# A Flamingo block on one core: the last two batches of the attention are finished in another way, and the first gate product is issued before a turn

## The chip, the cores and the metric

One core of one Trainium2 chip runs the whole program. The metric is the device time in microseconds of one execution, as the median of several runs. Engines: PE (matrix), DVE (vector), ACT (scalar), POOL (GpSimd), SP (issues DMAs).

## The reference, cut to what matters

x and ctx are (16, 256, 256), so there are 16 batches of 256 tokens and 256 features; 16 heads of 16.

```python
q = _layernorm(x) @ Wq.T + bq;  k = ctx @ Wk.T + bk;  v = ctx @ Wv.T + bv
attn = softmax(q k^T / 4)                  # per head
x = x + tanh(g_xattn) * ((attn v) @ Wo.T + bo)
h = act_qdq(_layernorm(x))                 # scale from the maximum over the whole tensor
up, gate = act_qdq(h @ W_up.T), act_qdq(h @ W_gate.T)
gate = act_qdq(gate * fixed_qdq_u16(sigmoid(gate)))
x = x + tanh(g_ffn) * (act_qdq(gate * up) @ W_down.T)
```

The maximum over the whole tensor in the first act_qdq is what splits the program in two: no gate product can start before the attention of all 16 batches and their second layernorm are done.

## The kernel before, in words

The program has two blocks with a barrier between them: `attention` (lines 29 to 810) and `feed_forward` (lines 892 on).

**Order of the attention.** Every engine walks through the same numbered steps g from -40 to 158, eight steps to a batch (`STEPS`, `batch(g, off)`: a task with offset off is done for batch b at step 8b + off). Nothing else sets the order; semaphores only make one engine wait for another. Scores for batch b are done one batch ahead, twice: `s_ps` (line 438, for the row maximum, taken on DVE in line 715) and, transposed, `st_ps` (line 453), which ACT turns into exponentials (line 606). From step 120 on there are no more `s_ps` scores, from step 128 on no more exponentials: the steps after that are the tail. Matmul inputs are split into a high and a low f16 part, so a product of two 256-wide operands (`split_product`) is 6 matmuls per 128 rows, 12 for a batch.

**The end of a batch.** `values` (line 412) multiplies the exponentials with the values at steps 2, 4, 6 and 8; each head takes 32 rows of `pv_ps`, 16 with its output, one with its denominator, 15 empty. ACT copies the two halves to `ot` at steps 5 and 9 (`take`, line 553). Then, for each batch b:

- step 10, SP: DMA of the denominators' rows from `ot` to `den` (line 336);
- step 12, DVE: reciprocal `rec` (line 753);
- step 14, SP: `rec` to DRAM (line 347), four DMAs that pack the second half's 16-row pieces of `ot` into the empty rows of the first (line 352), a DMA that reads the reciprocals from DRAM, each spread over 16 rows, into `recb` (line 357), and the load of `xr` (line 362);
- step 18, POOL: `at` = `ot` * `recb` (line 852); step 20, ACT: its f16 high part `ah` (line 632); step 21, DVE: the low part `al` (line 757);
- step 22, POOL: `xb`, the residual with the bias (line 868); step 23, PE: the output projection (line 467); step 24, DVE: `y` (line 725), SP: the store of y; step 25, DVE: statistics (lines 730, 735); step 26, POOL: `rstd` (lines 815, 817) and the normalised `lnall` (line 859), which is on DVE for the last two batches (line 742); step 30, DVE: the maximum (line 760).

After the last step the maximum over the partitions goes over PE twice (lines 542, 544) to `lmaxall` (line 809), and the barrier follows.

**Weights of the feed-forward.** They are quantised in pieces along the steps, turned on PE (`turn_weights`, 12 turns of 6 transposes each, through `s_ps`) and copied out by ACT (`keep_weights`, line 573), four at steps 131 and 132, four at 137, four at 139. A turn waits until the copy two before it is done.

**Start of the feed-forward.** DVE makes integers of `lnall` (line 1221), PE turns them (`turn`, line 1001), ACT and DVE split them (lines 1079, 1227); `gate(c, d)` on PE waits for the split of chunk c, turns chunk c + 2 and issues three pairs of products (line 1011) per chunk of two batches.

## Time and profile before

| | us |
|---|---|
| median of 3 runs (632.51 to 634.73) | 632.62 |
| the profiled execution | 634.7 |
| its span in the trace | 632.9 |
| PE busy | 567.9 (90%) |
| DVE busy | 486.7 (77%) |
| ACT busy | 437.5 (69%) |
| POOL busy | 202.0 (32%) |
| barrier between the blocks, about | 348 |

A row of the timeline has the start, the duration of the whole row, the engine, the line, the operation, output and input, and how many instructions it merges; in brackets stands the idle time ahead of it and what ended it. A row of windows has the length, then the busy time and the number of instructions for each engine, and PEclk, the granted clock of TensorE as a share of 2.4 GHz: 1.00 is 2.4 GHz and 0.50 is 1.2 GHz.

### The profile page before, as it was taken

What the parts mean: (1) busy time and instruction counts of PE and PEld (TensorE: products, weight loads), DVE (VectorE), ACT (ScalarE), POOL (GpSimd) and SP (SyncE); (2) the same over time, 40 slices, a digit from 0 to 9 for tenths busy, and PEclk for the clock granted to TensorE, in tenths of its full rate; (3) what the DMA queues carried; (4) which work ended last, traced back from release to release, by engine and by line L of the source; (5) the groups of instructions that cost most, each with busy time, mean ns of one, the idle gap of its engine ahead of it and who ended that gap; (6) DMA issues with size and microseconds to landing.
All of it is one profiled execution on the core that took longest, in us unless ns stands there. A gap on an engine that the chain in (4) does not pass through costs nothing. (4 is left out here: it accounts for less than half of the span.)

```text
span 632.9 us, 11543 instructions
## 1 busy us (share of the span) xinstructions
PE 567.9 (90%) x4271; PEld 338.0 (53%) x4271; DVE 486.7 (77%) x797; ACT 437.5 (69%) x629; POOL 202.0 (32%) x219
## 2 busy tenths in 40 slices
PE   2679999899999999999873799999999899949997
PEld 1346666566565666665442444434444344428886
DVE  5677889999999999898644298896888799964441
ACT  2226888678787787887762244437999998869960
POOL 4622347766665777653452000000000000010000
PEclk9879999999999999999986799999999999969999
DMA  6422444445435444333231000000000000013332
GB/s 189 126 85 76 129 127 129 120 138 143 147 112 136 141 128 110 111 106 106 63 83 54 2 1 0 1 1 0 1 0 1 1 1 0 1 66 101 135 134 99
DMA packets 42951, 49.12 MB, mean 78 GB/s; under 512 B 10640, under 2 KB 30480, under 8 KB 42896
## 3 DMA queue, kind: packets, MB, share of 16 engines
q1 hardware_dynamic: 41312, 43.81, 23.8%
q0 software_dynamic: 1152, 4.19, 2.1%
q8 instruction: 34, 0.56, 0.4%
q10 hardware_dynamic: 432, 0.39, 0.2%
q14 instruction: 21, 0.17, 0.1%
HBM read 24.58 MB, written 8.72 MB: 53 GB/s over the span
## 5 line engine op out<-in xcount | busy, mean ns | idle before, releaser
L715 DVE TENSOR_REDUCE negm<-s_ps 128x2 f32<-128x512 f32 x256 | 163.7, 682 | 28.2 <-PE s_ps L438 27.5
L606 ACT ACTIVATE pt<-st_ps 128x512 f32<-128x512 f32 x256 | 138.7, 596 | 56.1 <-PE st_ps L453 55.0
L1011 PE MATMUL pairs<-xq,wut 128*128 128x512 f16 x576 | 126.0, 379 | 6.5 <-DVE cmax L1276 3.4
L1011 PEld LDWEIGHTS pairs<-xq,wut 128*128 128x128 f16 x576 | 55.5, 98 | 77.0 <-DVE cmax L1276 7.3
L438 PE MATMUL s_ps<-kst,qst 96*128 96x256 f16 x512 | 82.9, 280 | 10.8 <-DVE negm L715 5.6
L453 PE MATMUL st_ps<-qst,kst 97*128 97x512 f16 x256 | 77.4, 383 | 0.8 <-ACT pt L606 0.8
L420 PE MATMUL pv_ps<-pt,vt 128*32 128x256 f32 x1024 | 68.5, 385 | 1.4 <-ACT ot L557 0.7
L1383 POOL PARTITION_ALL_REDUCE vmax<-vmax x5 | 1.8, 370 | 204.7 <-DVE vmax L1231 129.8
L1011 PE MATMUL pairs<-xq,wgt 128*128 128x512 f16 x288 | 65.0, 385 | 0.4 <-DVE xq L1227 0.3
L438 PEld LDWEIGHTS s_ps<-kst,qst 96*128 96x128 f16 x512 | 46.8, 99 | 34.0 <-DVE negm L715 21.2
L826 POOL TENSOR_SCALAR xn<-xt,mv,rstd 128x256 f32<-128x256 f32 x30 | 36.5, 1223 | 64.6 <-PE misc L518 64.4
L1064 PE MATMUL pairs<-wdt,h 128*128 128x256 f16 x384 | 48.9, 279 | 8.4 <-ACT h L1171 8.4
L1089 ACT COPY gb<-pairs 128x1024 f32<-128x1024 f32 x24 | 24.3, 1012 | 41.6 <-PE pairs L1011 41.6
L420 PEld LDWEIGHTS pv_ps<-pt,vt 128*32 128x32 f32 x1024 | 26.9, 109 | 38.7 <-issue 25.3
L1011 PEld LDWEIGHTS pairs<-xq,wgt 128*128 128x128 f16 x288 | 28.1, 99 | 34.6 <-issue 2.0
L1064 PEld LDWEIGHTS pairs<-wdt,h 128*128 128x128 f16 x384 | 38.3, 100 | 14.1 <-issue 8.8
L1283 DVE CUSTOM_DVE_ANT_0 gb<-lnall 128x1024 f32<-128x1024 int16 x24 | 29.1, 1217 | 13.5 <-ACT lnall L1118 13.5
L550 ACT ACTIVATE qk<-misc,bqk_s 128x256 f16<-128x256 f32 x64 | 26.9, 473 | 18.2 <-PE misc L381 18.2
L1244 DVE TENSOR_REDUCE cmax<-gb 128x1 f32<-128x3072 f32 (+1 forms) x10 | 27.1, 2710 | 15.5 <-ACT gb L1089 15.5
L859 POOL TENSOR_SCALAR lnall<-y,mv,rstd 128x256 f32<-128x256 f32 x28 | 34.0, 1221 | 1.5
L1367 DVE SCALAR_TENSOR_TENSOR lnall<-pairs,scal,lnall 128x512 f32<-128x512 f32 x16 | 11.9, 749 | 26.5 <-PE pairs L1064 26.5
L1135 ACT ACTIVATE lnall<-pairs,scal 128x1024 int16<-128x1024 f32 x24 | 26.5, 1112 | 6.4 <-PE pairs L1011 6.3
(164 smaller groups left out, 1026.7 us busy)
## 6 DMA issues: line engine op xcount, KB each, us to landing
qst<-qk SPq DMA_DIRECT2D x96, 64.0 KB, 2.1
kst<-qk SPq DMA_DIRECT2D x45, 128.0 KB, 3.2
xt<-in_x SPq DMA_DIRECT2D x16, 256.0 KB, 4.3
ct<-in_ctx SPq DMA_DIRECT2D x16, 256.0 KB, 3.1
recb<-rec_dram SPq DMA_DIRECT2D x16, 256.0 KB
xr<-in_x SPq DMA_DIRECT2D x16, 256.0 KB, 4.0
out<-y SPq DMA_DIRECT2D x16, 256.0 KB, 4.0
lnall<-out POOLq DMA_DIRECT2D x8, 512.0 KB, 4.3
```

The costliest lines, as they stand in the source:

```text
L420: mm = nc.tensor.matmul(pv_ps[32 * c:32 * c + 32, u % 2, :], vt[:, b % 3, kt, 8 * (c // 2) + 2 * u + c % 2, :], pt[:, u % 2, c // 2, kt, c ...
L438: mm = nc.tensor.matmul(s_ps[tt][:, r, :], qst[0:96, b % 3, r, j, tt * P:(tt + 1) * P], kst[0:96, b % 3, j, :], start=True, stop=True)
L453: nc.tensor.matmul(st_ps[u % 3][:], kst[:, b % 3, j, kt * P:(kt + 1) * P], qst[:, b % 3, :, j, :], start=True, stop=True).then_inc(st_done, 1)
L550: op = nc.scalar.activation(qk[:, 2 * i, e, :], frm[:, e, :], ACT.Identity, bias=bqk_s[:, i, e:e + 1])
L606: nc.scalar.activation(pt[:, (j // 2) % 2, j % 2, kt], st_ps[u % 3][:], ACT.Exp, scale=1.0 / (WS * WS * HD ** 0.5)).then_inc(exp_done, 1)
L715: nc.vector.tensor_reduce(negm[:, b % 2, tt, lo:lo + 5:4], s_ps[tt][:], AX.X, ALU.max, negate=True).then_inc(max_done, 1)
L826: op = nc.gpsimd.tensor_scalar(xn[:, tt, :], xt[:, b % 3, tt, :], mv[:, tt, 0:1], rstd[:, tt:tt + 1], ALU.subtract, ALU.mult)
L859: nc.gpsimd.tensor_scalar(t["lnall"][:, b, tt * D:(tt + 1) * D], y[:, b % 2, tt, :], mv2[:, tt, 0:1], rstd2[:, tt:tt + 1], ALU.subtract, A ...
L1011: mm = nc.tensor.matmul(ps[:, p, k, :], w[:, a, dt, f * P:(f + 1) * P], xq[:, b, c, dt, :], start=n == 0, stop=n == len(terms) - 1)
L1064: mm = nc.tensor.matmul(ps[:, 2 + d, b, tt * D:(tt + 1) * D], lh, wdt[:, h, f, :], start=n == 0, stop=n == len(terms) - 1)
L1244: nc.vector.tensor_reduce(cmax[:, 0, n:n + 1], tile, AX.XY, ALU.max).then_inc(g_max, 1)
L1283: nc.vector.tensor_tensor_reduce(gb[:, c, 2 * p:2 * p + 2].rearrange("p f w -> p (f w)"), ia[:, d, 2 * p:2 * p + 2].rearrange("p f w -> p ...
```

## The change

Batches are counted from 0; LAST is 15, END is step 128.

1. **Batch 15 without DMAs.** Its denominators no longer go through `den`, DRAM and `recb`. For each half v, PE multiplies four 128-column pieces of `ot` with four columns of the identity (`turn_den`), which puts the denominators on the partitions; DVE takes the reciprocal of 16 columns and copies it 32 wide (`rec_of`); PE turns that back (`turn_rec`, four f32 matmuls with 128 columns) into PSUM, spread over the rows; DVE multiplies it with `ot` (`attended`). Halves are not packed: each is cast (`high_last`, ACT; `low_last`, DVE) and projected by itself (`project_last`, 12 matmuls for each half) with a copy of Wo that has zeros in the rows without output (`wo16`). `y` and its statistics are made in two pieces.
2. **`wo16`** is prepared at steps 80 to 87 on POOL: a memset of 1024 columns and eight DMAs from POOL's queue, one per step.
3. **Batch 14.** SP packs it at step 122, right behind the load of `den`, ahead of the store of `rec` and the load of `recb` (step 123). POOL multiplies at step 127, ACT casts at step 128 ahead of `take(15, 1)`, DVE's low part and PE's projection follow at 128 and 129.
4. **Weights.** Turns 0 and 1 go between `turn_den(1)` and `turn_rec(1)`, turns 2 to 9 behind `project_last(1)`, turns 10 and 11 behind the first product of the final maximum. They go through `st_ps`. ACT's copies stand in the same order.
5. **Order on DVE at the end.** Normalising and maximum of batch 14 stand behind the statistics of batch 15; `mv2`, `ve2`, `rstd2` have two buffers.
6. **Feed-forward.** In `gate(0)` the first pair of products is issued before `turn(2, 0)`.

```diff
+            def store_rec(b): ...
+            def pack(b):
+                sp.wait_ge(den_loaded, 16 * (b + 1))
+                if b >= 2:
+                    sp.wait_ge(at_done, b - 1)
+                for c in range(4):
+                    sp.dma_start(ot[32 * c + HD:32 * c + 32, b % 2, 0], ot[32 * c:32 * c + HD, b % 2, 1]
+                                 ).then_inc(packed[b % 2], 16)
+            def spread_rec(b): ...
...
-                if (b := batch(g, 10)) is not None:
+                if (b := batch(g, 10)) is not None and b < LAST:
...
+                if g == END - 6:
+                    pack(LAST - 1)
+                if g == END - 5:
+                    store_rec(LAST - 1)
+                    spread_rec(LAST - 1)
...
+            def turn_den(v):
+                pe.wait_ge(ot_taken, 2 * LAST + v + 1)
+                frm = ot[:, LAST % 2, v].rearrange("p u q -> p (u q)")
+                for c in range(4):
+                    mm = nc.tensor.matmul(den_ps[:, 64 * v + 4 * c:64 * v + 4 * c + 4], frm[:, c * P:(c + 1) * P],
+                                          ident[:, HD:P:32], start=True, stop=True)
+                mm.then_inc(den_turned, 1)
+            def turn_rec(v):
+                pe.wait_ge(rec_wide, v + 1)
+                pe.wait_ge(at_last, v)
+                for c in range(4):
+                    mm = nc.tensor.matmul(recb_ps[:, c * P:(c + 1) * P], recx[:, c * P:(c + 1) * P], ident[:],
+                                          start=True, stop=True)
+                mm.then_inc(rec_spread, 1)
+            def project_last(v):
+                terms = [(x, w, k) for x, w in ((ahl[v], 0), (ahl[v], 1), (all_[v], 0)) for k in range(2)]
+                pe.wait_ge(ah_last, v + 1)
+                for first in range(2):
+                    if first == 1:
+                        pe.wait_ge(al_last, v + 1)
+                    for tt in range(KT):
+                        for m, (x, w, k) in list(enumerate(terms))[4 * first:4 + 2 * first]:
+                            mm = nc.tensor.matmul(last_ps[tt], x[:, k, tt * P:(tt + 1) * P], wo16[:, v, w, k, :],
+                                                  start=v == 0 and m == 0, stop=v == 1 and m == len(terms) - 1)
+                        if v == 1 and first == 1:
+                            mm.then_inc(o_last, 1)
...
+                if g == END - 2:
+                    pe.wait_ge(max_done, UNITS * NB)
+                    turn_den(0)
+                if g == END - 1:
+                    turn_rec(0)
...
-                if g in (PREP + 11, PREP + 12): ...
-                if g in (PREP + 17, PREP + 19): ...
+                if g == END + 1:
+                    project_out(LAST - 1, bank(PAIRS * (LAST - 1) + PROJ), g)
+                    turn_den(1)
+                    pe.wait_ge(ident16_set, 1)
+                    pe.wait_ge(exp_done, UNITS * NB)
+                    for k in range(2):
+                        turn_weights(0, k)
+                    turn_rec(1)
+                    pe.wait_ge(wo16_set, 128)
+                    project_last(0)
+                    project_last(1)
+                    for n in range(2, 10):
+                        turn_weights(n // 4, n % 4)
             pe.wait_ge(lmax_done, 1)
             pe.wait_ge(ot_taken, 2 * NB)
             nc.tensor.transpose(pv_ps[0:1, 0, 0:P], lmax[:], ident[:]).then_inc(lmax_turned, 1)
+            for k in range(2, 4):
+                turn_weights(2, k)
...
+                if g == END:                                  # ACT
+                    high_of(LAST - 1)
                 if (b := batch(g, 9)) is not None:
                     take(b, 1)
...
+                if g == END + 1:
+                    high_last(0)
+                    keep_weights(0, 0)
+                    keep_weights(0, 1)
+                    high_last(1)
+                    for n in range(2, 12):
+                        keep_weights(n // 4, n % 4)
...
+                if g == END - 1:                              # DVE
+                    rec_of(0)
+                if g == END:
+                    low_of(LAST - 1)
+                    attended(0)
+                if g == END + 1:
+                    rec_of(1)
+                    low_last(0)
+                    y_of(LAST - 1)
+                    attended(1)
+                    stats_of(LAST - 1)
+                    low_last(1)
+                if g == END + 7:
+                    for tt in range(KT): ...                  # y and bn_stats of each piece
+                    gather_stats(LAST)
+                    ln_last(LAST - 1)
+                    ln_max(LAST - 1)
+                    ln_last(LAST)
+                    ln_max(LAST)
...
+                if g == 80:                                   # POOL
+                    nc.gpsimd.memset(wfall[:].rearrange("p n t d -> p (n t d)")[:, 0:4 * D], 0.0).then_inc(wo16_zeroed, 1)
+                if 80 <= g < 88:
+                    v, c = divmod(g - 80, 4)
+                    pool.dma_start(wo16[32 * c:32 * c + HD, v], wo2[32 * c + HD * v:32 * c + HD * v + HD]).then_inc(wo16_set, 16)
...
             def gate(c, d):
                 pe.wait_ge(xt_low, c + 1)
-                if ahead(c, 2):
+                if c and ahead(c, 2):
                     turn(c + 2, d)
                 for p in range(PR):
+                    if c == 0 and p == 1:
+                        turn(2, 0)
                     pe.wait_ge(g_kept, PR * c + p + 1)
                     products(wgt, c, p).then_inc(g_done, 1)
```

## Rows read from the trace of the kernel before

**Rows 1.** Busy time by stretch: four windows (us), granted clock, DMA share, GB/s.

```profile
211.00:228.40 17.40, 17.40 (x169) 11.39 (x167) 15.96 (x34) 13.49 (x29) 12.38 (x14) 1.00 0.51 145
...
330.00:332.00 2.00, 1.21 (x18) 0.90 (x15) 1.69 (x5) 1.58 (x3) 0.00 (x0) 0.98 0.61 95
336.00:338.00 2.00, 0.00 (x0) 0.00 (x0) 1.71 (x3) 0.86 (x2) 1.49 (x2) 0.73 0.00 0
356.00:358.00 2.00, 2.00 (x7) 0.74 (x6) 0.00 (x0) 0.00 (x0) 0.00 (x0) 0.65 0.00 0
```

**Rows 2.** Timeline of PE at the end of the attention block.

```profile
327.19 0.58 PE L381 MATMUL misc<-woh,ah 128*128 128x256 f16 x2 [1.25 <-DVE al L757]
...
338.82 0.58 PE L381 MATMUL misc<-woh,ah 128*128 128x256 f16 x2 [3.31 <-DVE al L757]
...
346.21 0.37 PE L542 MATMUL pv_ps<-ident,lmax 128*1 128x128 f32 x1 [4.68 <-DVE lmax L805]
```

**Rows 3.** Timeline of DVE at the end of the attention block.

```profile
326.31 0.63 DVE L757 TENSOR_TENSOR al<-at,ah 128x512 f16<-128x512 f32 x1
...
336.30 1.67 DVE L742 TENSOR_SCALAR lnall<-y,mv,rstd 128x256 f32<-128x256 f32 x2 [4.53 <-POOL rstd L817]
...
341.58 0.75 DVE L725 SCALAR_TENSOR_TENSOR y<-misc,tgs,xb 128x512 f32<-128x512 f32 x1 [2.42 <-PE misc L381]
...
344.50 0.73 DVE L742 TENSOR_SCALAR lnall<-y,mv,rstd 128x256 f32<-128x256 f32 x2 [1.10 <-POOL rstd L817]
...
347.57 0.16 DVE L809 COPY lmaxall<-pv_ps 128x1 f32<-128x1 f32 x1 [0.67 <-PE pv_ps L544]
```

**Rows 4.** Timeline of ACT at the end of the attention block.

```profile
323.31 0.59 ACT L557 COPY ot<-pv_ps 128x512 f32<-128x512 f32 x1 [1.47 <-PE pv_ps L420]
...
325.17 0.64 ACT L632 CAST ah<-at 128x512 f16<-128x512 f32 x1
...
330.42 2.98 ACT L573 COPY wut<-s_ps 128x768 f16<-128x768 f16 x4 [3.21 <-PE s_ps L409]
```

**Rows 5.** Timeline of SP's queue, the last batch but one.

```profile
313.54 0.59 SPq L336 DMA_DIRECT2D den<-ot  x1
316.01 0.32 SPq L347 DMA_DIRECT2D rec_dram<-rec  x1
316.43 2.45 SPq L352 DMA_DIRECT2D ot<-ot  x4
318.99 0.66 SPq L357 DMA_DIRECT2D recb<-rec_dram  x1
```

**Rows 6.** DMA issues from 300 to 345 us: KB each, median us to landing.

```profile
rec_dram<-rec SPq DMA_DIRECT2D x3, 16.0 KB, 1.4
```

**Rows 7.** Timeline of POOL, the last two batches.

```profile
323.37 1.27 POOL L852 TENSOR_TENSOR at<-ot,recb 128x512 f32<-128x512 f32 x1 [3.88 <-DMA recb<-rec_dram]
...
336.23 1.26 POOL L868 TENSOR_TENSOR xb<-xr,tbo 128x512 f32<-128x512 f32 x1
```

**Rows 8.** Line 496: weight loads of its f32 matmuls, duration min/median/max ns, first and last start.

```profile
L496 PEld LDWEIGHTS pv_ps<-wof,bvw x4: 186/190/190, 19.0 to 19.5; 128*128 128x128 f32 x4
```

**Rows 9.** Line 776 on DVE: a copy with a broadcast input, duration min/median/max ns.

```profile
L776 DVE COPY bvw<-bvc x1: 1384/1384/1384, 17.5 to 17.5; 128x256 f32<-128x256 f32 x1
```

**Rows 10.** Timeline of all engines where the feed-forward block starts.

```profile
349.97 1.89 PE L1001 MATMUL pairs<-ident,h 128*128 128x128 f16 x16 [2.44 <-DVE h L1221]
...
352.09 0.69 DVE L1227 TENSOR_TENSOR xq<-pairs,xq 128x1024 f16<-128x1024 int16 x1 [1.39 <-ACT xq L1079]
...
353.59 1.01 PE L1001 MATMUL pairs<-ident,h 128*128 128x128 f16 x8 [1.73 <-DVE h L1221]
```

**Rows 11.** Line 1392: software DMA issues on POOL, min/median/max ns.

```profile
L1392 POOL DMA_DIRECT2D lnall<-out x8: 722/722/1021, 561.3 to 617.2; - x8
```

**Rows 12.** Timeline of POOL and PE in the steady state, near step 80.

```profile
228.62 1.15 POOL L846 TENSOR_TENSOR cl<-ct,ch 128x512 f16<-128x512 f32 x1
...
232.03 0.38 PE L381 MATMUL misc<-ch,wh_k 128*128 128x256 f16 x2
```

More of the change, by code:

```diff
@@ L466, in _ @@
                     mm.then_inc(v_done, 1)
[L467 to L478 removed]
+                if (b := batch(g, PROJ)) is not None and b < LAST - 1:
+                    project_out(b, bank(g), g)
                 if (b := batch(g, Q)) is not None:
@@ L628, in _ @@
                     nc.scalar.copy(ch[:], ct[:, b % 2]).then_inc(ch_done, 1)
-                if (b := batch(g, 20)) is not None:
-                    act.wait_ge(at_done, b + 1)
-                    act.wait_ge(o_done, b)
-                    nc.scalar.copy(ah[:], at[:, b % 2]).then_inc(ah_done, 1)
+                if (b := batch(g, 20)) is not None and b < LAST - 1:
+                    high_of(b)
                 if g == -13:
@@ new lines, in low_of, with rec_row, ln_last @@
+            def low_of(b):
+                dve.wait_ge(ah_done, b + 1)
+                dve.wait_ge(o_done, b)
+                nc.vector.tensor_tensor(al[:], at[:, b % 2], ah[:], ALU.subtract).then_inc(al_done, 1)
+            def rec_row(b):
+                dve.wait_ge(den_loaded, 16 * (b + 1))
+                if b:
+                    dve.wait_ge(rec_written, 16 * b)
+                nc.vector.reciprocal(rec[:], den[:]).then_inc(rec_done, 1)
+            def ln_last(b):
+                dve.wait_ge(rstd2_done, b + 1)
+                for tt in range(KT):
+                    nc.vector.tensor_scalar(t["lnall"][:, b, tt * D:(tt + 1) * D], y[:, b % 2, tt, :], mv2[:, b % 2, tt, 0:1],
+                                            rstd2[:, b % 2, tt:tt + 1], ALU.subtract, ALU.mult).then_inc(ln_done, 1)
@@ L738, in _ @@
                     low(0, bank(PAIRS * b + Q), ql_done)
-                if (b := batch(g, 26)) is not None and b >= NB - 2:
-                    dve.wait_ge(rstd2_done, b + 1)
-                    for tt in range(KT):
-                        nc.vector.tensor_scalar(t["lnall"][:, b, tt * D:(tt + 1) * D], y[:, b % 2, tt, :], mv2[:, tt, 0:1],
-                                                rstd2[:, tt:tt + 1], ALU.subtract, ALU.mult).then_inc(ln_done, 1)
                 if (b := batch(g, -29)) is not None and b >= 3:
@@ new lines, in _ @@
+                if (b := batch(g, 30)) is not None and b < LAST - 1:
+                    ln_max(b)
+                if g == END - 1:
[10 more added lines that the diff above has]
+                    low_last(1)
```

237 lines of the change are left out of this document (147 added, 90 removed).

## The prediction

> **What bounds the kernel now.** I read the page's slices first, then windows, then the timeline of each engine from 310 to 360 us, where nearly all of the change lies. In the steady state PE has no gap at all: 17.40 us busy of 17.40 for one batch, with POOL at 12.38 [rows 1]. What matters there is only whether PE is made to wait. In the tail no engine is full; a chain of hand-overs decides. Look at PE: it sits idle for 1.25 us ahead of the projection of batch 14 and 3.31 us ahead of that of batch 15, each time waiting for the low part from DVE, and 4.68 us ahead of the final maximum [rows 2]. Behind the waits stands a DMA: POOL waited 3.88 us for `recb` of batch 14 [rows 7]. From the last copy of `pv_ps` (323.31 + 0.59 = 323.90) [rows 4] to the projection of batch 15 (338.82) [rows 2] it takes 14.9 us, for some 6 us of work. From there to the end of the last DVE operation, 347.57 + 0.16 = 347.73 [rows 3], it is 8.9 us, and the barrier follows. Whatever moves the last engine's end at this barrier moves the whole feed-forward by as much. TensorE's clock is the second thing to see: after the gap behind the weight turns it falls to 1.2 GHz (0.73 between 336 and 338) and is back at 2.4 GHz only between 356 and 358; after the shorter gap at 326 it had fallen as well, since two matmuls took the same 0.58 us at 327.19 as at 338.82 [rows 2], and from 330 to 332 it was up again at 0.98 [rows 1].
>
> **Batch 14, the new start of the chain.** `den` was issued at 313.54 and the reciprocal was there when `rec` was issued at 316.01; the four packs took SP 2.45 us and `recb` went out at 318.99 [rows 5]. Now the packs come first: they can start when `den` has landed, about 315.65, and hold SP until 318.1. Only then does the store of `rec` go, lands 1.4 us later [rows 6] at about 319.6, and `recb` follows at 319.65, 0.65 us later than before. Before, 323.37 - 318.99 = 4.4 us passed until POOL had it [rows 5, 7]; I take the same, since `xr` still follows at once. So POOL starts at 324.0 instead of 323.37 and ends at 325.3. (Bounds: without the packs' traffic beside it `recb` could land 1 us sooner; it could also land 1 us later.) ACT casts, 0.64 us [rows 4], until 325.95, and only then does `take(15, 1)`, 0.59 us, until 326.5. PE's side reaches that point by about 325.4: `turn_den(0)` and `turn_rec(0)` add some 3 us to its queue ahead of `values(15, 3)`, and ACT's wait covers them by 0.5 us; without that cover they would cost up to 1 us. DVE's low part takes 0.63 us [rows 3], so PE's projection of batch 14 starts at 326.8 (before 327.19, [rows 2]). At 1.2 GHz its twelve matmuls start 0.213 us apart (338.82 to 341.4 for the other one, y begins at 341.58, [rows 2, 3]), so it ends at 329.4.
>
> **Batch 15, second half.** `turn_den(1)`: four f32 matmuls are eight passes, since line 496 shows four weight loads for two matmuls, 0.19 us each [rows 8]. 8 x 0.19 = 1.5, and 0.2 until it can be read: 331.1. Reciprocal 0.3. The copy 32 wide is 512 columns from one source; the nearest rows are 0.73 / 2 = 0.37 us for 256 columns of one-source work [rows 3] and 1.384 for a 256-column copy with a broadcast input [rows 9]. Lower end 0.6, upper 2 x 1.38 = 2.8. I take 0.9, nearer to the lower end, since it is the same kind of work, with something added because POOL is at work on batch 13's `lnall` here: 332.4. `turn_rec(1)` 8 x 0.19 + 0.15: 334.1. `attended(1)` 0.7: 334.9. ACT casts until 335.5; DVE has the statistics of batch 14 (1.05 us) in between and has the low part at 336.65. PE has done `project_last(0)` and two thirds of `project_last(1)` by then (about 1.3 and 0.9 us if the clock is up since 330, as it was before) and needs four more matmuls: the last starts at about 337.1, and both pieces are there at 337.45. Before, that point was 341.58 [rows 3]. So the join comes **4.1 us earlier**.
>
> **What is late next.** `y`, statistics, aggregation, the root on POOL (1.10 us of idle on DVE, [rows 3]) and the maximum took 347.73 - 341.58 = 6.15 us. Now batch 14's normalising and maximum (0.73 + 0.69) fall into the root's wait and stick out by 0.4, and batch 13's maximum adds 0.3 ahead of y. How long such work takes beside POOL is open: the two normalising operations of batch 14 took 1.67 us together, beginning at 336.30 beside POOL's `xb` (336.23, 1.26 us), those of batch 15 only 0.73; `al` took 0.63 at 326.31, with POOL at work too [rows 3, 7]. In my sum that does not matter yet (rival E prices it), because another chain ends later: **the weights**. Before, turns and copies lay inside the waits and cost nothing. Now ten of twelve copies come after `project_last(1)`. One is 2.98 / 4 = 0.745 us on ACT [rows 4]. From 337.15: first turn 0.5, ten copies 7.45, end 345.1. DVE's chain would end at 337.45 + 6.15 + 0.7 = 344.3, and 0.3 more because the last small matmul stands behind turn 11 in PE's queue: 344.6. So ACT ends the block at 345.1 against 347.73: **-2.6 us**.
>
> **Feed-forward.** PE waited for the integers of chunk 2 and started its turn at 353.59, though DVE's split for chunk 0 was done at 352.09 + 0.69 = 352.78 [rows 10]. With the product first, PE works from 352.82: **-0.77 us**. The turn itself is the same work later. If the clock rises at the same moment whatever PE does, half of that is lost (-0.4).
>
> **Steady state.** POOL gets a memset (about 0.9) and eight DMA issues of 0.72 to 1.02 us [rows 11]: 6.7 to 9.1 us against 17.40 - 12.38 = 5.0 us of idle per batch [rows 1]. It runs 1.7 to 4.1 us late and recovers in the next batch. Who waits: `cl` is done at 229.77 and PE needs it at 232.03 [rows 12], 2.26 us of slack against 0.9 + 0.72 ahead of it. I take 0; upper end 2.
>
> **Sum.** -2.6 - 0.8 = -3.4 us. Against the profiled execution, 634.7 (span 632.9), that is 631.3 (span 629.5). The median of the runs shown is 632.62, 2.1 us below that execution, so the forecast is **629.2 us**.
>
> **Rivals.**
> - *A, the join comes late.* The clock stays at 1.2 GHz from 326.8 to the join, which makes `turn_den`, `turn_rec` and the two last projections about 2.6 us longer; a wide copy near its upper end or a late `recb` would do the same. Everything behind moves with it: 345.1 + 2.6 = 347.7, where the block ended before, and only the feed-forward's 0.8 is left: **631.8**. For it: PE idles until 326.8, and the clock was down in that place [rows 2]. Against: it rose after that with PE as busy as here.
> - *B, the clock stays up.* Weight turns fill PE until the barrier, as they did up to 336 when it was at 2.4 GHz. If it is still up at the first turn, the 3.8 us from 353.59 to about 357.4 at 1.2 GHz take 1.9, and the first turns 0.4 less: **627.0**. Against: about 2.9 us of PE idle around the barrier (its last matmul near 344.4, its first turn 349.97 - 347.73 = 2.24 us behind the last engine's end, [rows 3, 10]), and the clock fell in the gap after 336 [rows 1].
> - *C, slower: POOL's software DMAs.* Place: steps 80 to 87. If an issue holds POOL 2 us and more instead of 0.72, POOL is 8 x 2 + 0.9 = 16.9 us fuller, 11.9 beyond its idle time, and PE waits for `cl` and the `at` chain for all but 2.3 of it: +9.6 - 3.4, **638.8**. It makes the kernel slower from 1.2 us per issue on. For it: the only price is that of another shape [rows 11].
> - *D, POOL's lateness is paid once.* The issues cost what the row shows, but `cl` or the `at` chain has less slack than I think and PE waits for the upper end of 2 us: **631.2**.
> - *E, DVE is held by POOL and its chain ends the block.* If normalising batch 14 beside POOL's root takes 1.67 instead of 0.73 us (+0.9), and the wide copy and the low part ahead of the join are held for another 0.6 together, DVE ends at 344.6 + 1.5 = 346.1 instead of ACT at 345.1: **630.2**. For it: 1.67 beside `xb`; against: `al` at 0.63 [rows 3, 7]. The Trainium skill (GPSIMD Engine Reference, Specifications) says that POOL's SBUF interfaces are shared with VectorE, with contention for DVE instructions in a two-port mode or with two SBUF inputs. By that rule both kinds of work are held here and E is what comes; by the row of `al` only the normalising is, and the sum stays as it is. The trace agrees for one of the two kinds.
>
> **Chances.** Forecast 0.44 (own range 627.9 to 630.6), A 0.18, B 0.12, C 0.06, D 0.10, E 0.10. No change can be told within 0.5%, 3.16 us, so the forecast lies just beyond that line; of its 0.44 I give 0.27 to faster, 0.17 to same, and of E 0.03 and 0.07. Faster 0.27 + 0.12 + 0.01 of A + 0.03, same 0.17 + 0.17 + 0.10 + 0.07, slower 0.06. The range runs from B with some spread, 626.3, to A and D with theirs, 632.7.
>
> **What would show it.** Steps: `at` of batch 14 at 324 and not before 323.4; `take(15, 1)` behind the cast; y of batch 15 near 337.5; ten ACT copies of 0.745 us in a row as the last thing before the barrier; PE's products 2.85 us after its first turn. Wrong: if DVE or PE ends the block, if `values(15, 3)` is later than ACT's cast, if the copy 32 wide takes over 1.5 us, if PE shows gaps between 228 and 250 us, or if the granted clock is 1.00 at the first turn of the feed-forward.

## Result and the profile after

The changed kernel takes **626.91 us** (median of 4 runs, 624.88 to 627.51) against 632.57 us before (median of 4 runs, 632.18 to 634.73). The ratio is 0.9899, 95% interval 0.9875 to 0.9923. That is faster by over 0.5%, but the gain is 5.7 us where the sum said 3.4. The time lies inside the whole range of the forecast (626.3 to 632.7), yet outside the forecast's own (627.9 to 630.6): it falls in the part that belonged to rival B, and rival B's condition, a clock that is still up at the first turn of the feed-forward, was not met. So that it is inside is luck. Of all the runs below one, 632.52 us of the kernel e4, was in a slower state and is left out of that kernel's ratio.

The two profiled executions differ by more, 632.9 and 623.0 us of span, and one has to see first how much of these 9.9 us the change can have made. I cut both at the same events. The work ahead of the first copy of `pv_ps` ended 3.55 us earlier, though the change touches none of it: over all profiles below that point lies anywhere between 54.6 and 59.4 us, 58.35 before and 54.80 after (last section). From there to the end of batch 9 it took 0.8 us less (170.47 and 169.64). Nothing of the change is known to act there, yet the three profiles of kernels with the old tail (before, e1, e5) have 170.3 to 170.5 us and the eleven others 169.6 to 170.1, with no overlap. Some 0.5 us of it may therefore belong to the change in a way that no run explains. What is left lies where the change acts:

| stretch (us) | before | after | difference |
|---|---|---|---|
| batches 10 and 11 | 35.13 | 36.26 | +1.13 |
| issue of `den` (14) to first DVE operation of the feed-forward | 35.01 | 30.06 | -4.95 |
| from there to the end | 284.35 | 282.66 | -1.69 |

Their sum, -5.5, fits the medians, with the 0.5 us or without. One profile of each kernel is a thin base for the last line: over the six profiles of kernels with the changed feed-forward and no idle matmuls (after, a0, e2, e3, e6, e7) it is 282.7 to 283.7 us, 283.2 in the mean, so the gain there is nearer to 1.2 than to 1.7 us. First the windows of the kernel after, which answer to [rows 1]: length, busy time and number of instructions of PE, PEld, DVE, ACT, POOL, then granted clock, DMA share and GB/s.

```profile
222.40:239.80 17.40, 17.21 (x165) 11.24 (x165) 16.39 (x35) 13.99 (x31) 15.48 (x19) 1.00 0.47 132
239.80:257.20 17.40, 16.81 (x163) 11.12 (x156) 15.26 (x34) 13.93 (x30) 13.56 (x16) 1.00 0.42 121
...
322.00:324.00 2.00, 0.00 (x0) 0.00 (x0) 0.81 (x1) 1.10 (x2) 1.73 (x2) 1.00 0.70 201
340.00:342.00 2.00, 0.46 (x5) 0.46 (x6) 1.59 (x4) 0.00 (x0) 0.00 (x0) 0.62 0.02 4
344.00:346.00 2.00, 1.60 (x4) 0.58 (x5) 2.00 (x5) 0.54 (x1) 0.00 (x0) 0.50 0.00 0
346.00:348.00 2.00, 2.00 (x8) 0.76 (x7) 0.28 (x1) 0.00 (x0) 0.54 (x1) 0.67 0.00 0
348.00:350.00 2.00, 2.00 (x17) 1.17 (x16) 0.00 (x0) 1.01 (x1) 0.00 (x0) 1.00 0.00 0
```

Three things are to be seen. PE, gapless in [rows 1], lacks 0.19 and 0.59 us in the two batches in which POOL issues the new DMAs. The clock stays at 2.4 GHz (1.00) through the whole tail, also in the window in which PE did nothing. It falls only at the barrier and is back about 7 us behind the first DVE operation of the feed-forward (340.34), where before it took 9 us from 348.55 [rows 1].

PE's timeline at the end, which answers to [rows 2] (start, duration, engine, line, operation, idle time ahead and what ended it):

```profile
324.53 0.60 PE L416 MATMUL misc<-wo,ah 128*128 128x256 f16 x4 [2.63 <-DVE al L830]
...
325.84 0.95 PE L478 MATMUL s_ps<-ident,ot 128*128 128x4 f32 x8
326.65 0.83 PE L444 MATMUL st_ps<-ident,wut 128*128 128x128 f16 x12
327.88 1.16 PE L486 MATMUL s_ps<-ident,wi 128*128 128x128 f32 x8 [0.40 <-DVE wi L813]
...
331.36 0.39 PE L499 MATMUL misc<-wfall,cl 128*128 128x256 f16 x2
...
331.81 0.83 PE L444 MATMUL st_ps<-ident,wut 128*128 128x128 f16 x12
...
341.54 1.89 PE L1179 MATMUL pairs<-ident,h 128*128 128x128 f16 x16 [2.32 <-DVE h L1401]
344.40 4.18 PE L1189 MATMUL pairs<-xq,wgt 128*128 128x512 f16 x12 [0.98 <-DVE xq L1407]
```

The projection of batch 14 (324.53) lasts 1.31 us until `turn_den(1)` at 325.84, at 2.4 GHz; I had 2.6. DVE and ACT in the same stretch, for [rows 3] and [rows 4]:

```profile
323.19 1.09 DVE L830 TENSOR_TENSOR al<-at,ah 128x512 f16<-128x512 f32 x1 [2.39 <-ACT ah L662]
...
326.83 0.26 DVE L809 RECIPROCAL recl<-s_ps 128x16 f32<-128x16 f32 x1 [1.01 <-PE s_ps L478]
327.18 0.65 DVE L813 COPY wi<-recl 128x512 f32<-128x512 f32 x1
...
329.08 0.69 DVE L819 TENSOR_TENSOR at<-ot,s_ps 128x512 f32<-128x512 f32 x1
...
331.82 0.47 DVE L913 SCALAR_TENSOR_TENSOR y<-misc,tgs,xb 128x256 f32<-128x256 f32 x1
...
333.81 0.70 DVE L841 TENSOR_SCALAR lnall<-y,mv,rstd 128x256 f32<-128x256 f32 x2
...
339.26 0.16 DVE L971 COPY lmaxall<-pv_ps 128x1 f32<-128x1 f32 x1 [1.40 <-PE pv_ps L623]
```

```profile
322.54 0.62 ACT L662 CAST ah<-at 128x512 f16<-128x512 f32 x1 [2.94 <-POOL at L1014]
323.06 0.58 ACT L636 COPY ot<-pv_ps 128x512 f32<-128x512 f32 x1
...
332.35 1.50 ACT L652 COPY wgt<-st_ps 128x768 f16<-128x768 f16 x2 [1.92 <-PE st_ps L444]
333.82 2.98 ACT L652 COPY wut<-st_ps 128x768 f16<-128x768 f16 x4
336.77 2.98 ACT L652 COPY wdt<-st_ps 128x768 f16<-128x768 f16 x4
```

`take(15, 1)` stands behind the cast, as foreseen. The join (y of batch 15, first piece) is at 331.82. DVE has the last maximum at 339.42, 7.60 us behind it; ACT's copies run without a gap until 339.75, 7.93 us behind it. So ACT ends the block, as the sum had it, and DVE is 0.3 us from doing so.

SP and POOL (batch 14), for [rows 5] and [rows 7]:

```profile
310.28 0.59 SPq L376 DMA_DIRECT2D den<-ot  x1
312.60 2.46 SPq L330 DMA_DIRECT2D ot<-ot  x4
315.10 0.58 SPq L323 DMA_DIRECT2D rec_dram<-rec  x1
316.79 0.66 SPq L337 DMA_DIRECT2D recb<-rec_dram  x1
```

```profile
321.24 1.27 POOL L1014 TENSOR_TENSOR at<-ot,recb 128x512 f32<-128x512 f32 x1 [4.42 <-DMA recb<-rec_dram]
322.46 1.27 POOL L1019 TENSOR_TENSOR xb<-xr,tbo 128x512 f32<-128x512 f32 x1
```

`recb` goes out 6.51 us behind `den`, against 5.45 before, and POOL starts at 10.96 against 9.83.

### The profile page after: what moved, and what is told of

The parts are those of the page before. It is cut to its first block and busy times, and to the rows that moved or that the text cites. A ratio compares the mean times of both kernels' runs of the same rounds, so it can differ in the third digit from the quotient of the medians.

```text
span 623.0 us, 11662 instructions
## 1 busy us (share of the span) xinstructions
PE 565.0 (91%) x4315; PEld 338.5 (54%) x4315; DVE 488.8 (78%) x804; ACT 438.4 (70%) x630; POOL 206.7 (33%) x227
## 5 line engine op out<-in xcount | busy, mean ns | idle before, releaser
L695 ACT ACTIVATE pt<-st_ps 128x512 f32<-128x512 f32 x256 | 138.8, 596 | 54.6 <-PE st_ps L531 53.5
L516 PE MATMUL s_ps<-kst,qst 96*128 96x256 f16 x512 | 81.1, 275 | 11.0 <-DVE negm L872 7.2
L1502 DVE TENSOR_TENSOR gb<-lnall 128x1024 f32<-128x1024 int16 x24 | 29.1, 1215 | 2.4 <-ACT lnall L1319 2.4
```

Source lines behind the costliest of these rows:

```text
L516: mm = nc.tensor.matmul(s_ps[tt][:, r, :], qst[0:96, b % 3, r, j, tt * P:(tt + 1) * P], kst[0:96, b % 3, j, :], start=True, stop=True)
L695: nc.scalar.activation(pt[:, (j // 2) % 2, j % 2, kt], st_ps[u % 3][:], ACT.Exp, scale=1.0 / (WS * WS * HD ** 0.5)).then_inc(exp_done, 1)
L1502: nc.vector.tensor_tensor(gb[:, c, 2 * p:2 * p + 2], ia[:, c % 2, 2 * p:2 * p + 2], ib[:, c % 2, 2 * p:2 * p + 2], ALU.mult).then_inc(p3_d ...
```

## The experiments

Each run's profile was cut at the same events. In this table of the tail the times count from the issue of `den` for batch 14, in us. The last line is the stretch from the feed-forward's first DVE operation to the end.

| | before | after | a0 | e3 | e6 | e4 | e5 | b2 |
|---|---|---|---|---|---|---|---|---|
| `recb` issued | 5.45 | 6.51 | 6.66 | 5.45 | 6.62 | 6.12 | 5.45 | 5.46 |
| `at` (14) starts | 9.83 | 10.96 | 10.37 | 9.42 | 10.95 | 10.03 | 9.26 | 9.67 |
| `take(15, 1)` starts | 9.77 | 12.78 | 12.21 | 13.19 | 12.79 | 11.87 | 9.76 | 11.51 |
| join | 28.04 | 21.54 | 20.97 | 20.21 | 21.56 | 20.63 | 26.41 | 20.29 |
| first DVE op. of feed-forward | 35.01 | 30.06 | 29.48 | 28.72 | 28.93 | 29.14 | 33.09 | 28.10 |
| rest of the program | 284.35 | 282.66 | 283.21 | 283.74 | 283.42 | 280.15 | 285.74 | 280.97 |

The join is the first operation of the last `y`. The names in the table are those of the runs below. Each ratio is taken against runs of the kernel before that were made at the same time (medians 633.4, 633.72 and 633.0 us for three groups of kernels). No run puts back the main edit alone, batch 15 without DMAs; what it brings is read from the chain in the profiles.

**The changed kernel again.**

> The changed kernel once more, as the anchor for the others. Theory: its gain is in three places, tail of the attention about -5.0 us (from the issue of den of batch 14 to the first DVE operation of the feed-forward, 30.1 us against 35.0), feed-forward about -1.7, and POOL's DMAs in batches 10 and 11 +1.1, so 626.9 in the median. The 3.55 us that its first profiled execution was ahead before the first copy of pv_ps (54.80 against 58.35) belong to the clock at the start and not to the change: here the first copy should lie anywhere between 54 and 60 us. Rival: they belong to the change (nothing in it acts before step 80), then the first copy is at 54.8 again and the median nearer to 624.

Measured: 626.9 us (6 runs), ratio 0.9902 (0.9875 to 0.9929). The tail is the first profile's within 0.6 us, the difference being when `recb` landed. So the clock that is up at the projection of batch 14 is no accident of one execution: it was at 2.4 GHz there in all eleven profiles of the changed kernel and of its variants. The clock came back 7.7 us behind the first DVE operation of the feed-forward, not 7.0, and the rest of the program took 283.21 us.

**Only the order of the feed-forward**, in the kernel before:

```diff
-                if ahead(c, 2):
+                if c and ahead(c, 2):
                     turn(c + 2, d)
                 for p in range(PR):
+                    if c == 0 and p == 1:
+                        turn(2, 0)
```

> The kernel before with only the feed-forward part of the change: the first pair of products ahead of turn(2, 0). Theory: PE starts its products right behind DVE's split, 0.77 us sooner, and since the clock is at 1.2 GHz there for some time behind the start it wins 0.4 to 0.8: 631.9 to 632.2. Rival: PE's work only swaps places and the later turn holds chunk 2, no gain within 0.2 us.

Measured: 632.33 us (12 runs), ratio 0.9984 (0.9967 to 1.0002), that is -1.0 us and hardly told from nothing. Its profile shows why this term is less than it looks: the windows about its first product (PE's work from 350 us) are

```profile
350.00:352.00 2.00, 2.00 (x6) 0.65 (x5) 1.72 (x4) 0.00 (x0) 0.77 (x1) 0.50 0.00 0
352.00:354.00 2.00, 2.00 (x6) 0.71 (x5) 0.00 (x0) 0.00 (x0) 0.00 (x0) 0.50 0.00 0
354.00:356.00 2.00, 2.00 (x14) 1.12 (x13) 0.00 (x0) 0.81 (x1) 0.00 (x0) 0.69 0.00 0
356.00:358.00 2.00, 2.00 (x11) 0.94 (x10) 0.00 (x0) 0.20 (x1) 0.00 (x0) 1.00 0.00 0
```

PE works without a gap, but at 1.2 GHz, and DVE's first maximum over the products came 16.39 us behind the first DVE operation, against 16.34 before, with the clock back at +9.7 instead of +8.8. The loss from the later rise is half of 0.9, so by this working, which no run separates, the order itself gives about 0.4 us.

**POOL's DMAs.** In one kernel they were spread, two at a time, over steps 83 to 107, with the memset at 83; in another they were left out (the memset stays, so batch 15 is projected with zeros and the output is not the reference's).

```diff
-                if 80 <= g < 88:
-                    v, c = divmod(g - 80, 4)
+                if g in (83, 91, 99, 107):
+                    for n in ((g - 83) // 4, (g - 83) // 4 + 1):
+                        v, c = divmod(n, 4)
```

> The eight DMAs that fill wo16 go two at a time to steps 83, 91, 99 and 107, just ahead of the place where POOL waited 4.6 us for PE, with the memset at 83. Theory: POOL's lateness in steps 80 to 88 makes PE wait once, 1.1 us in all between the copies of batches 10 and 11; spread out it costs nothing, so 1.1 us faster than the changed kernel, 625.8. Rival: the 1.1 us come from elsewhere (load of the queue, a phase of PE and DVE), then the same time as the changed kernel within 0.3 us.

> The changed kernel without the eight DMAs from POOL's queue that fill wo16 (the memset stays, so the last batch is projected with zeros and its output is not the reference's). Theory: these DMAs hold POOL for 6 us in batch 10 and the PE waits once for it, so the stretch from the second copy of batch 9 to that of batch 11 goes from 36.26 back to 35.13 us and nothing is paid later: 1.1 us faster than the changed kernel. Rival: spread over four batches they only moved the loss behind batch 11 (50.5 instead of 49.6 us up to den), so it is a loss of phase between PE and DVE that comes back wherever POOL is late, and it is gone here altogether; if even here the stretch or the one behind it is long, it is not the DMAs.

Measured: spread 626.46 us (6 runs), ratio 0.9900 (0.9872 to 0.9927); left out 625.53 us (4 runs), 0.9877 (0.9855 to 0.9899). Without the DMAs batches 10 and 11 take 35.13 us, as before, and the stretch behind them 49.59, again as before. Spread, the first is 35.13 but the second 50.50: the cost had moved, 0.9 us of it, not gone. (b1, which has this edit too, takes 50.90 there; the twelve kernels without it 49.6 to 50.2, so that stretch varies by some 0.6 us by itself.) The medians of the three kernels can't be told apart; it is the stretches that show the cost. How it comes about is seen on POOL in the changed kernel, behind batch 10:

```profile
236.55 2.42 POOL L988 TENSOR_SCALAR xn<-xt,mv,rstd 128x256 f32<-128x256 f32 x2 [0.74 <-PE misc L591]
238.92 1.07 POOL L1047 DMA_DIRECT2D wfall<-wo  x2
240.01 1.28 POOL L1036 TENSOR_TENSOR xb<-xr,tbo 128x512 f32<-128x512 f32 x1
```

and then on DVE and on PE of the same kernel:

```profile
241.38 0.75 DVE L789 SCALAR_TENSOR_TENSOR y<-misc,tgs,xb 128x512 f32<-128x512 f32 x1 [1.29 <-issue]
```

```profile
228.00 0.38 PE L416 MATMUL misc<-ch,wh_k 128*128 128x256 f16 x2 [0.19 <-POOL cl L1008]
...
242.19 0.39 PE L416 MATMUL misc<-xh,wh_q 128*128 128x256 f16 x2 [0.59 <-DVE y L789]
```

Without the DMAs PE has no such wait from 224 to 245 us, and the same operations stand so (POOL, then DVE):

```profile
238.45 1.27 POOL L1036 TENSOR_TENSOR xb<-xr,tbo 128x512 f32<-128x512 f32 x1
```

```profile
239.81 0.75 DVE L789 SCALAR_TENSOR_TENSOR y<-misc,tgs,xb 128x512 f32<-128x512 f32 x1 [0.20 <-issue]
```

Two issues stand between `xn` and `xb`. Counted from the second copy of batch 9, `xb` starts 1.44 us later with them (15.57 and 14.13). DVE's y needs `xb` and starts 0.09 us behind its end in both kernels, and PE's next product needs the bank that y reads. This chain had less slack than `cl`, for which PE waited only 0.19 us. The two gaps make 0.78 of the 1.13 us; where the other 0.35 lie I can't show.

**Packing batch 14 behind the store again:**

```diff
-                if g == END - 6:
-                    pack(LAST - 1)
                 if g == END - 5:
                     store_rec(LAST - 1)
+                    pack(LAST - 1)
                     spread_rec(LAST - 1)
```

> Only the order on SP's queue for batch 14 is put back: the reciprocals are stored first, then the four packs, then recb. Theory: packing first delays recb from 5.45 to 6.51 us behind den, and the whole chain hangs on it: at of batch 14 starts 10 us behind den instead of 10.96, the join and the barrier come about 1 us earlier, 625.9. Rival: recb lands when the packs' traffic is through, whatever is issued first, or take(15, 1) is held by PE's values at 321.9 instead; then within 0.3 us of the changed kernel.

Measured: 626.14 us (6 runs), ratio 0.9894 (0.9866 to 0.9921), not told from the changed kernel. The profile tells more: `recb` goes out at 5.45 again, `at` starts 1.0 to 1.5 us earlier and the join comes 0.8 to 1.3 earlier than in the two profiles of the changed kernel. It is not the whole 1.5, because now PE's side of `take(15, 1)` is late: in this execution the clock was down for 3.4 us, and PE took 1.94 us for what had been 1.07 (first line). `values(15, 3)` (second line) then ended at 325.16, and `take(15, 1)` started at 325.23. It began 12.05 us behind `den` instead of 10.55; in e2, which packs first but whose clock fell in the same place, it is 12.05 as well, so this lateness goes with the clock and not with the edit.

```profile
318.91 1.94 PE L454 MATMUL pv_ps<-pt,vt 128*32 128x256 f32 x16
...
324.09 1.07 PE L454 MATMUL pv_ps<-pt,vt 128*32 128x256 f32 x16
```

So packing first bought nothing here; it cost about 1 us of chain. In the profiled execution what was gained in the tail was lost again behind it: the feed-forward's clock came back 8.5 us behind its first operation instead of 6.95, and the rest took 283.74 us. Whether that holds for the other runs, whose median did not move, is not shown.

**Half of the weights ahead of the join** (PE's part; ACT's copies follow the same order):

```diff
                 if g == END - 1:
+                    turn_weights(0, 0)
+                    turn_weights(0, 1)
                     turn_rec(0)
...
+                    turn_weights(0, 2)
+                    turn_weights(0, 3)
                     project_out(LAST - 1, ...)
                     turn_den(1)
-                    for k in range(2):
-                        turn_weights(0, k)
+                    turn_weights(1, 0)
+                    turn_weights(1, 1)
                     turn_rec(1)
...
-                    for n in range(2, 10):
+                    for n in range(6, 12):
```

> The changed kernel with six of the twelve weight turns and copies in ACT's gaps: two ahead of turn_rec(0), two ahead of the projection of batch 14, two behind turn_den(1); the other six behind project_last(1), none behind the final transpose. Theory: the ten copies of 0.74 us behind the join end the block at 339.75 and DVE's chain would end at 338.3; with six left (4.5 us) DVE decides: 1.4 us faster than the changed kernel, 625.5. Rival: the copies delay the casts on ACT's queue, or the turns the values of batch 15 on PE, by as much: no gain within 0.3 us.

Measured: 627.0 us (6 runs), ratio 0.9898 (0.9878 to 0.9918). The block does end earlier: with six copies left ACT is done 4.97 us behind the join, DVE's chain 6.54 (7.60 in the changed kernel, since PE's small matmuls no longer stand behind a turn), and the feed-forward starts 7.37 us behind the join, where the changed kernel and the five variants that keep its ten copies and its small matmuls (a0, e2, e3, e4, e7) all have 8.51 or 8.52.

```profile
335.80 2.98 ACT L654 COPY wdt<-st_ps 128x768 f16<-128x768 f16 x4
```

But PE's last weight turn now ends at 337.94, 3.2 us ahead of the feed-forward's first operation; the clock falls 2.4 us ahead of that operation instead of with it, and is back at +7.9. The rest of the program took 283.42 us, 0.8 longer than in the first profile of the changed kernel but only 0.2 longer than in its second, so that the gain is given back in this way is likely and not shown; the median says only that it is not there. What is shown is that the weights ended the block and that the chain on DVE is right behind them.

**Idle matmuls at the barrier.** They compute nothing that is read:

```diff
+            def idle_work(n):
+                for i in range(n):
+                    nc.tensor.matmul(ps[:, 2, 0, :], wgt[:, 0, 0, 0:P], wut[:, 0, 0, 0:CW], start=True, stop=True)
+            idle_work(5)
             turn(0, 0)
             turn(1, 1)
+            idle_work(5)
```

> Five idle 512-column matmuls of no use ahead of the first turn of the feed-forward and five behind the second, into a bank that is not in use yet. Theory: the clock falls to 1.2 GHz at about 340.5, 1.3 us after PE's last work, and is back at 347.3; filling the gaps from 340.2 on keeps it up, and half of the time that PE works at 1.2 GHz (about 1.0 us of turns and 2.9 us of products) comes back: 1.5 to 1.9 us faster, 625.2. Rival: the gap around the barrier (339.25 to 340.3) cannot be filled and is enough to drop the clock; then the idle matmuls run at 1.2 GHz and delay the first turn by up to 0.9 us: 627.5, with the clock back a little sooner.

> Idle matmuls as in the kernel that filled the gaps at the start of the feed-forward, and two more behind the last small matmul of the attention, under ACT's last copy. Theory: the clock never falls around the barrier, the first reduction of the feed-forward starts 13.1 us behind its first DVE operation instead of 15, and what is behind it is the same; from the first DVE operation to the end 280.2 us against 282.7 to 283.2: 2.7 us faster than the changed kernel, 624.2, in every execution. Rival: the clock falls in some executions all the same, then the idle matmuls delay the first turn and the time is as unsteady as before.

Measured: 626.21 us (6 runs), ratio 0.9871 (0.9841 to 0.9900); with two more behind the last small matmul of the attention (e8), 624.43 us (4 runs, 623.84 to 624.79), ratio 0.9861 (0.9839 to 0.9882). In both profiles the clock stays at 1.00 over the barrier, the first maximum over the products comes 13.12 us behind the first DVE operation instead of 14.95, and the rest of the program takes 280.15 and 280.78 us. In all four profiles in which idle matmuls kept the clock up (e4, e8 and, below, b2 and b3) it takes 280.2 to 281.6 us, in the six profiles of the same code without them 282.7 to 283.7. The window at the start of the feed-forward, with the first five of them (e4):

```profile
344.00:346.00 2.00, 1.59 (x12) 0.78 (x13) 1.48 (x4) 0.00 (x0) 0.00 (x0) 1.00 0.01 4
```

By this the clock at the feed-forward's start is worth 2 to 2.5 us in the changed kernel; the medians (2.0 and 2.6 us by the ratios) agree, though their intervals overlap with the changed kernel's. The runs of e4 in its ratio scatter over 4.4 us (623.08 to 627.46), those of e8 over 1 us. Perhaps the clock still fell in some runs of e4; no profile shows one, and it stays open.

**Idle matmuls in the tail of the kernel before** (4 ahead of the projection of batch 14, 12 ahead of that of batch 15, 20 ahead of the final maximum):

```diff
+                if g == PREP + 12:
+                    idle_work(4)
...
+                if g == PREP + 19:
+                    idle_work(12)
+            idle_work(20)
             pe.wait_ge(lmax_done, 1)
```

> The kernel before with idle 512-column matmuls in three gaps of PE in the tail (4 behind the weight turns of step 132, 12 behind the last weight turn, 20 behind the projection of batch 15), into a bank without use, so that the clock does not fall. Theory: the clock's part of the gain is separate from that of the DMAs: the projection of batch 15 takes 1.3 us instead of 2.6, the barrier comes 1.3 us sooner, and nothing else moves: 631.3. Rival: the projection is not what the end hangs on (the store of y or the weights are), or the idle matmuls push the projection back: no gain or 0.5 us lost.

Measured: 631.68 us (12 runs), ratio 0.9981 (0.9961 to 1.0001). The join came 1.6 us earlier, the feed-forward 1.9. Not all of the 1.6 is the clock's: `at` of batch 15 started 20.01 us behind `den` instead of 20.38, though its `recb` was issued at the same 15.87. The projection of batch 15, from its first product (337.87) to y, took 1.51 us instead of 2.76, and that is the clock's. But the clock fell at the barrier, later than in the kernel before, and rose later (second fence, windows):

```profile
337.87 0.38 PE L381 MATMUL misc<-woh,ah 128*128 128x256 f16 x2 [1.73 <-DVE al L769]
```

```profile
352.00:354.00 2.00, 2.00 (x6) 0.66 (x5) 0.21 (x1) 0.00 (x0) 0.41 (x1) 0.50 0.00 0
...
356.00:358.00 2.00, 2.00 (x9) 0.83 (x8) 0.00 (x0) 0.91 (x1) 0.00 (x0) 0.81 0.00 0
```

Counted from the first DVE operation, 346.06 us in that execution, the clock is back at +10.7 and the first maximum stands at 17.25 instead of 16.34: 0.9 of the 1.9 us was lost there. The 1.0 that is left agrees with the ratio (-1.2 us, whose interval just reaches no change); the whole rest of the program, 1.4 us longer, would leave 0.5. In the tail of before the clock was worth about 1.25 us; the change brings the join forward by 6.5, so most of that is the chain itself.

**Combinations.** b1 is e2, e3, e4 and e6 together. b3 is e3 and e8 with `turn_rec(0)` moved behind `values(15, 3)`. b2 is b3 with two more turns and copies ahead of the join (four in all), and with idle matmuls at two places ahead of the barrier, one and three instead of two:

```diff
                 if g == END:
+                    turn_weights(0, 0)
+                    turn_weights(0, 1)
+                    turn_rec(0)                                # was ahead of values(15, 3)
...
                     turn_den(1)
-                    for k in range(2): turn_weights(0, k)
+                    turn_weights(0, 2)
+                    turn_weights(0, 3)
                     turn_rec(1)
...
             nc.tensor.transpose(...).then_inc(lmax_turned, 1)
-            for k in range(2, 4): turn_weights(2, k)
+            idle_work(1)
             nc.tensor.matmul(pv_ps[:, 1, 0:1], ...).then_inc(ltop_spread, 1)
+            idle_work(3)
```

> The four edits together: DMAs spread, store of the reciprocals first, six weight turns early, idle matmuls at the start of the feed-forward. Theory: they act in different places and add up, 1.1 + 1.0 + 1.4 + 1.7: 5 us faster than the changed kernel, 621.7. Rival: with recb earlier, PE's values(15, 3) and ACT's early copies become the bound, and the idle matmuls give nothing: 1.5 to 2.5 us faster, 624.5 to 625.5.

> The changed kernel with: reciprocals of batch 14 stored first, turn_rec(0) behind the values of batch 15, four of the twelve turns and copies ahead of the join, idle matmuls on both sides of the barrier. Theory: recb leads, PE's values no longer do, so take(15, 1) ends 11.9 us behind den instead of 12.2 to 12.8, the join is at 19.9, DVE and ACT end the block together 6.5 behind it, and the clock stays up: 27.3 us to the first DVE operation of the feed-forward and 280.2 from there, 622.0. Rival: the clock falls around the barrier, as in the version with six turns early: 624.

> The same without the earlier weight turns. Theory: the ten copies behind the join end the block 7.9 behind it and keep PE at work until the barrier: join at 19.9, 28.3 to the first DVE operation, 280.2 from there: 623.0, one us slower than with four turns early. Rival: steadier clock makes it the faster of the two.

Measured: b1 624.34 us (5 runs), ratio 0.9852 (0.9831 to 0.9874). b2 **623.5 us** (4 runs), ratio **0.9847** (0.9823 to 0.9872). b3 625.65 us (5 runs), ratio 0.9877 (0.9856 to 0.9899). Each missed its own expectation of the time by 1.5 to 2.7 us. b2 has the lowest median of all and beats both kernels; b1 can't be told from it, though its idle matmuls ran at 1.2 GHz and its rest took 283.31 us, which shows that idle matmuls bring nothing when they come too late: the clock had fallen 2 us ahead of the feed-forward's first operation, where PE had no weight turns left. In b2's profile PE has no gap over 0.7 us from 316 to 345 us, and the clock stays at 2.4 GHz on both sides of the barrier:

```profile
336.37 0.27 PE L624 MATMUL pv_ps<-ident,lmax 128*1 128x128 f32 x1
336.48 0.38 PE L474 MATMUL s_ps<-wo 128*128 128x512 f16 x1
337.02 0.38 PE L627 MATMUL pv_ps<-ltop,row 1*128 1x1 f32 x2 [0.16 <-DVE ltop L976]
337.33 0.82 PE L474 MATMUL s_ps<-wo 128*128 128x512 f16 x3
338.45 1.24 PE L1202 MATMUL pairs<-wut,wgt 128*128 128x512 f16 x5 [0.30 <-PEq L56]
339.93 1.28 PE L1186 MATMUL pairs<-ident,h 128*128 128x128 f16 x16 [0.24 <-DVE h L1414]
341.05 1.24 PE L1202 MATMUL pairs<-wut,wgt 128*128 128x512 f16 x5
342.38 2.76 PE L1196 MATMUL pairs<-xq,wgt 128*128 128x512 f16 x12
```

The twelve products take 2.76 us instead of 4.18, and the first turns 1.28 instead of 1.89. Its eight remaining ACT copies and DVE's chain end at nearly the same time (6.45 and 6.67 us behind the join).

## Why the prediction was right in direction and wrong in size

The order of the chain and which engine ends it were right; the chain's length was not.

- **Packs first.** Forecast: `recb` 0.65 later, `at` at 10.46 us behind `den`. Measured: 1.06 and 10.96. The packs began 0.2 us later behind `den` than I had them, and `recb` went out 1.69 us behind the store of `rec`, where I had 1.55. The 4.4 us from there to POOL held (4.45).
- **The step that failed: from `at` of batch 14 to the join** (the end of "Batch 14, the new start of the chain" and all of "Batch 15, second half"). From POOL's start (324.0 in the forecast) to the join (337.45) the text has 13.45 us; its sums hold to 0.1 us. The changed kernel took **10.58**, and a0, e4, e6 and b2 10.60 to 10.62. In the profiles in which the clock had fallen ahead of this stretch it was 10.8 to 11.3 (e2, e3, e7, e8, b3) and 12.1 (b1), less than forecast in every one. Term by term: ACT's cast and the low part, 0.5 longer than forecast; the projection of batch 14, taken at 1.2 GHz as [rows 2] show it, 1.31 instead of 2.6 us; `turn_den` 0.99 up to the reciprocal instead of 1.7; reciprocal and wide copy about 1.05 instead of 1.3; `turn_rec` 1.2 instead of 1.7; from there, `attended`, cast, low part and last projection, 2.74 instead of 3.35. The clock made the largest of these; twice eight f32 passes, which I took from the weight loads of [rows 8] at 0.19 us each, made the next: they ran at 0.12 (`turn_den`, 0.95 us) to 0.15 (`turn_rec`, 1.16 us), at 2.4 GHz as in [rows 8]. The join is 6.5 us earlier instead of 4.1.
- **The clock in that step.** I carried the fall of [rows 1, 2] over to a gap in the same place. PE's gap was 2.63 us, longer than the 1.25 in which the clock had fallen before, and the clock stayed. So the length of the one gap does not tell it; the work ahead of it differs too, and what decides was not separated and stays open. Rival A, which let the clock cost more, had its sign wrong: the error lay on the other side, and no rival held that case for the tail.
- **The weights** as the end of the block: forecast 7.65 us behind the join, measured 7.93. Right, shown by ACT's rows and by e6. Rival E did not come: the chain on DVE, 0.45 us longer than forecast, was still 0.3 us shorter than ACT's. The rule it draws on, that POOL's SBUF interfaces are shared with VectorE (the Trainium skill, GPSIMD Engine Reference, Specifications), is borne out, also for the work with two SBUF inputs, for which I had seen no sign. `al`, with its two SBUF inputs, took 0.68 us alone and 0.63 to 0.90 beside POOL's `lnall`, but 1.09 beside POOL's `xb` (323.19 and 322.46 above). In all 21 rows of the last 60 us of the attention, over twelve of the profiles, in which `al` began with 0.1 us or more of `xb` still to run, it ended 0.54 to 0.56 us behind the end of `xb`, and took up to 1.74 us: it looks as if it waits and is not slowed. The kernel before had such a row too, at 305.64 (0.85 us, beside `xb` from 304.68), outside the stretch that I showed. The copy 32 wide took 0.65 beside `lnall` against 0.43 for half 0. Both lie ahead of the join and are paid in the 10.58 us; the normalising of batch 14 (0.70) ran with hardly any work of POOL beside it.
- **Feed-forward.** Forecast -0.77, measured -1.69 in the first profile and -0.6 to -1.4 in the five others. The first product came 2.86 us behind the first turn, as foreseen (2.85). The order gives some 0.4 (e1, by the working there), and the clock, back at +6.95 instead of +8.8, half of the 1.85 us between, 0.9; the other 0.4 us is within the variation of that stretch. In the other five profiles the clock came back at +7.2 to +8.5. Rival B needed the clock up at the first turn; that did not happen in the changed kernel, but e4, e8, b2 and b3, which force it, gain about the 2.3 us it priced.
- **Steady state.** Forecast 0, upper end 2; measured +1.13, removed by e7. The slack of `cl` that I read in [rows 12] was about right, and it was the wrong chain: `xb` with y behind it had less. Rival D named the cost, but not where it falls; the gap in PE at 242.19 is one of the signs of being wrong that I had named, and it came.

So the errors are -2.3 us in the tail (-2.4 of it in the join), -0.9 in the feed-forward and +1.1 in the steady state, together -2.1 us on a forecast of -3.4; the medians give -5.7. The cost in the steady state hid a part of the miss: two errors of opposite sign, which is luck again.

## What to carry to other kernels

A chain of small matmuls should be priced at both clock levels, and the lower one needs more evidence than one gap of like length: the range, not the sum, is the place for it. Where PE waits at a barrier, a few matmuls that nobody reads can pay (here 2 to 2.5 us of 627), provided they start before the clock has fallen, as b1 shows by not keeping it up; and an edit that empties PE ahead of the barrier can bring that fall forward, as e6 does. When work is added to an engine with idle time, check every chain through it for slack, not the one whose number is at hand.

## What the runs showed of the hardware

- The clock did not fall over 2.63 us without PE work in the changed kernel (window 322 to 324: PE 0.00, clock 1.00), but had fallen around gaps of 1.25 and 3.31 us in the kernel before.
- It also fell with no gap over 0.81 us ahead: for about 3.4 us each time, beginning 21 to 23.5 us ahead of the feed-forward, during or right behind f32 products, in some executions (e2, e3, b1, b3, e7, e8) and not in others (after, a0, e4, e6, b2). It costs 0.9 us on the row of e3 (1.94 instead of 1.07), and there it lies on the path.
- VectorE's subtraction with two SBUF inputs, begun while POOL's `xb` ran, ended 0.54 to 0.56 us behind the end of `xb` in each of 21 rows, whether 0.1 or 1.0 us of `xb` had passed; alone it took 0.68 us.
- The start of the program, the same work in all kernels, varies by 4.8 us between profiles. In the windows 30 to 40 and 40 to 50 us the clock is 0.83 and 0.99 after, 0.67 and 0.67 before. The clock is not all of it: e2, with 0.83 in each window from 20 to 50 us, has its first copy at 58.14, and e5, with 0.66 to 0.71, at 57.56. What else sets it is open. Two single profiles should be compared from a common event on.
- Software DMAs of 16 rows from POOL took 0.48 to 0.83 us each to issue in the changed kernel, against 0.72 to 1.02 in [rows 11].
